# Tanh values of the mixing rounded once and spread to MT's row groups by DMA

## What is computed

```python
xx = x_prev - x
mix = jnp.tanh((x + xx * time_maa_x) @ maa_w1).reshape(b, t, 5, E_MIX)   # E_MIX = 32
mix = jnp.einsum('btfe,fec->fbtc', mix, maa_w2)
mw, mk, mv, mr, mg = mix
xw = x + xx * (time_maa_w + mw)      # and so for k, v, r, g
...
r, k, v = xr @ Wr.T, xk @ Wk.T, xv @ Wv.T
g = silu(xg @ Wg.T)
decay = exp(-exp(time_decay + tanh(xw @ td_w1) @ td_w2))
# a recurrence over time with decay, k, v and r; then a norm by head, times g, @ Wo.T
```

## Time and profile before

| | us |
|---|---|
| median of 3 runs | 3111.87 |
| lowest and highest run | 3108.07, 3113.85 |
| span of the profiled execution | 3113.6 |
| TensorE busy | 2943.4 (95%) |
| VectorE busy | 2445.0 (79%) |
| ScalarE busy | 1976.6 (63%) |
| GpSimd busy | 894.4 (29%) |
| ScalarE's copies into MT (L693), 330 | 135.6 |
| GpSimd's subtractions into MT (L905), 330 | 318.5 |

### The profile page before, as it was taken

The page is one execution under the profiler, slowest core; times in us unless marked ns, Lnnn a source line. Parts: engine busy times, 40 slices in busy tenths (PEclk is TensorE's granted clock), DMA queues, the critical chain, the costliest instruction groups (busy, mean ns, idle before and its releaser), DMA issues.

```text
span 3113.6 us, 102428 instructions
## 1 busy us (share of the span) xinstructions
PE 2943.4 (95%) x40633; PEld 2187.3 (70%) x40633; DVE 2445.0 (79%) x5275; ACT 1976.6 (63%) x4175; POOL 894.4 (29%) x790
## 2 busy tenths in 40 slices
PE   1889999999999999999999999999999999999997
PEld 0667777777777777677777777777777777777775
DVE  8467887787887787787778787778788778788777
ACT  0456676666677666677666667666667666667764
POOL 1223221333222233322233322233322233322222
PEclk9899999999999999999999999999999999999998
DMA  5000000000000000000000000000000000000000
GB/s 212 8 15 22 13 23 19 22 15 22 12 23 19 22 15 22 16 19 19 22 15 22 22 12 19 22 17 21 22 12 23 19 22 15 22 12 23 19 22 14
DMA packets 22823, 73.40 MB, mean 24 GB/s; under 512 B 3105, under 2 KB 3361, under 8 KB 20769
## 3 DMA queue, kind: packets, MB, share of 16 engines
q1 hardware_dynamic: 22432, 67.10, 6.3%
HBM read 50.31 MB, written 16.78 MB: 22 GB/s over the span
## 4 chain that ended last, share of the span: by engine, by line
PE 70%; DVE 19%; issue 6%; ACT 3%; DMA 1%; DVEq 1%; SPq 0%; ACTq 0%; POOLq 0%; POOL 0%
PE psP L402 18%; PE psF L636 11%; PE psP L440 7%; PE psP L611 7%; PE psF L663 6%; DVE HLO L1342 4%; PE psW L479 2%; PE psY L533 2%; PE psY L521 2%; DVE SUMS L1334 2%; PE psW L496 2%; PE psF L652 2%; DVE ARENA L1091 2%; DVE ARENA L1169 1%; DVE ARENA L1279 1%
## 5 line engine op out<-in xcount | busy, mean ns | idle before, releaser
L402 PE MATMUL psP<-ARENA,WALL 128*128 128x256 f32 x3072 | 698.7, 383 | 39.4 <-ACT ARENA L736 39.4
L693 ACT ACTIVATE ARENA<-ARENA 32x512 f32<-32x512 f32 (+3 forms) x1026 | 584.4, 570 | 221.2 <-DVE ARENA L1169 92.4
L402 PEld LDWEIGHTS psP<-ARENA,WALL 128*128 128x128 f32 x3072 | 573.7, 191 | 117.5 <-ACT ARENA L736 42.4
L1342 DVE SCALAR_TENSOR_TENSOR HLO<-GG,FWB,HHI 128x128 f16<-128x128 f32 x1024 | 347.6, 400 | 321.4 <-ACT HHI L864 316.3
L636 PE MATMUL psF<-XHI,WFC 128*128 128x128 f16 x4096 | 488.5, 220 | 1.9 <-DVE ST L1356 1.9
L636 PE MATMUL psF<-XLO,WFC 128*128 128x128 f16 x4096 | 487.1, 220 | 0.0
L905 POOL TENSOR_TENSOR MT<-ARENA 32x256 fp32r<-32x256 f32 x330 | 318.5, 965 | 467.3 <-ACT ARENA L693 438.7
L919 POOL TENSOR_TENSOR ARENA<-ARENA,XT 128x1024 f32<-128x1024 f32 x128 | 278.7, 2178 | 533.9 <-DVE ARENA L1103 533.9
L636 PEld LDWEIGHTS psF<-XHI,WFC 128*128 128x128 f16 x4096 | 398.3, 98 | 37.7 <-issue 32.9
L636 PEld LDWEIGHTS psF<-XLO,WFC 128*128 128x128 f16 x4096 | 402.0, 98 | 17.9 <-issue 10.3
L663 PE MATMUL psF<-WPJ,HHI 128*128 128x512 f16 x1024 | 390.9, 382 | 14.4 <-ACT GG L855 14.4
(11 more groups left out here) (165 smaller groups left out, 5242.1 us busy)
## 6 DMA issues: line engine op xcount, KB each, us to landing
XT<-x_ch SPq DMA_DIRECT2D x33, 520.0 KB, 3.4
ARENA<-x_tok SPq DMA_DIRECT2D x32, 512.0 KB, 3.5
out<-OUT SPq DMA_DIRECT2D x64, 256.0 KB, 2.1
WALL<-w_all SPq DMA_DIRECT2D x5, 1024.0 KB, 15.3
ARENA<-wfc SPq DMA_DIRECT2D x4, 1024.0 KB, 8.0
ARENA<-wpj SPq DMA_DIRECT2D x3, 1024.0 KB, 14.7
GG<-wpj SPq DMA_DIRECT2D x1, 1024.0 KB, 18.7
OUT<-w2a SPq DMA_DIRECT2D x8, 64.0 KB, 14.0
```

The lines of the kernel that those rows point to most:

```text
L402: mm = pe.matmul(psP[:, P.bank(f"{name}{g}"), COLS * c:COLS * (c + 1)], WALL[:, w, k, 128 * (2 * g + c):128 * (2 * g + c + 1)], cc(XF[slot ...
L693: return act.activation(o, i, ACT.Copy)
L1342: e = dve.scalar_tensor_tensor(out=HLO[:, k, :], in0=GG[:, u % 2, 0, 128 * m:128 * (m + 1)], scalar=FWB[:, 0, k:k + 1], in1=HHI[:, k, :], ...
```

## The change

ScalarE keeps the tanh and the two roundings (TMH, TMBH) and makes no copies into MT. GpSimd makes one subtraction of 128 x 256 (TML) and one of 32 x 256 (TMBL). SP issues eight DMAs per tile (`spread`), four of 128 KB from TMH and TML into groups 0 to 3 of MT[0..3], and four of 32 KB from TMBH and TMBL into those of MT[4]. TensorE waits for all four of the first kind before any of blends 0 to 3, and for all four of the second kind before blend 4. For a DMA whose destination has 32 partitions and four blends on each, the source must have the blends of one row next to each other; so GpSimd puts W1's 128 columns in that order once, in the prologue (w1_ordered), from a raw copy in V. TMBH and TMBL move to RM.

```diff
@@ -145,14 +145,15 @@
         A = ARENA1[:, 6144:7168]
         RSX = A.rearrange("p (q n) -> p q n", q=PAIRS)
         K1 = ARENA1[:, 7168:8192]
-        TMA, TMH = K1[:, 0:COLS], K1[:, COLS:2 * COLS]
-        TMB, TMBH = K1[0:MIXR, 2 * COLS:3 * COLS], K1[0:MIXR, 3 * COLS:4 * COLS]
+        TMA, TMH, TML = (K1[:, COLS * i:COLS * (i + 1)] for i in range(3))
+        TMB = K1[0:MIXR, 3 * COLS:4 * COLS]
         KT = ARENA1[:, 7168:8192].rearrange("p (q n) -> p q n", q=PAIRS)
         S = ARENA2[:, 0:512].rearrange("p (c b n) -> p c b n", b=B, c=KC)
         XF = [ARENA2[:, 512 + 1024 * i:1536 + 1024 * i] for i in range(2)]
         YSB, YSQ = XF
         KM = ARENA2[:, 2560:3584]
         RM = ARENA2[:, 3584:4608]
+        TMBH, TMBL = RM[0:MIXR, 0:COLS], RM[0:MIXR, COLS:2 * COLS]
         XTOK = KM.rearrange("p (h c) -> p h c", h=PAIRS)
         D = ARENA2[:, 4608:5632]
         G = ARENA2[:, 5632:6656]
@@ -194,6 +195,7 @@
         RAW = ([ARENA1[:, 2048 * k:2048 * (k + 1)] for k in range(4)] + [ARENA2[:, 2048 * k:2048 * (k + 1)] for k in range(3)]
                + [GG[:, :, :, :].rearrange("p i s n -> p (i s n)")])
 
+        W1RAW = V[:, 1, :].rearrange("p (k n) -> p k n", k=KC)
         W2RAW = (OUT[:, 0:2, :], X1[:, 0:2, :], V[:, 0:1, :])
         psP = ctx.enter_context(nc.psum_tensor("psP", [128, 2, 512], F32))
         psW = ctx.enter_context(nc.psum_tensor("psW", [128, 2, 512], F32))
@@ -215,7 +217,8 @@
         f_stats, f_product = sem("f_read_stats"), sem("f_read_product")
         y_full, y_copied, y_squared = sem("y_full"), sem("y_copied"), sem("y_squared")
         xx_ready, xm_ready, xf_ready = sem("xx_ready"), sem("xm_ready"), sem("xf_ready")
-        tm_rounded, mt_high, mt_low, w2_split = sem("tm_rounded"), sem("mt_high"), sem("mt_low"), sem("w2_split")
+        tm_rounded, tm_rest, w2_split, w1_ordered = sem("tm_rounded"), sem("tm_rest"), sem("w2_split"), sem("w1_ordered")
+        mt_first, mt_last = sem("mt_first_in"), sem("mt_last_in")
         gate_tanh, d_ready = sem("gate_tanh"), sem("d_ready")
         k1_even, k1_odd = sem("k1_even"), sem("k1_odd")
         rb_act, rb_dve = sem("rb_act"), sem("rb_dve")
@@ -262,7 +265,7 @@
                     halves(RM[rows(h), :], n)[1].rearrange("p (c q) n -> p c q n", c=KC))
 
         NPL = len(LEVELS) + 2
-        NWEIGHTS = 8 + 5 * 4
+        NWEIGHTS = 9 + 5 * 4
 
         def over_tiles(eng, attention, feed_forward):
 
@@ -286,7 +289,7 @@
                 sp.dma_start(RAW[4 + k], wpj[:, 2048 * k:2048 * (k + 1)]).then_inc(raw_in[4 + k], 16)
             sp.dma_start(XT[:, :, :], x_ch[0]).then_inc(xt_in, 16)
             sp.dma_start(WALL[:, W_V, :, :], w_all[:, W_V, :, :]).then_inc(values_in, 16)
-            for dst, src in ((W1[:, :, :], w1), (TD1[:, :, :], td1),
+            for dst, src in ((W1RAW, w1[:, :, 0:4 * MIXR]), (W1[:, :, 4 * MIXR:], w1[:, :, 4 * MIXR:]), (TD1[:, :, :], td1),
                              (TD2[0:DECR, :], td2), (TD2[DECR:2 * DECR, :], td2), (WALL[:, W_K, :, :], w_all[:, W_K, :, :])):
                 sp.dma_start(dst, src).then_inc(weights_in, 16)
             for f in range(5):
@@ -296,6 +299,25 @@
                 sp.dma_start(WALL[:, w, :, :], w_all[:, w, :, :]).then_inc(weights_in, 16)
 
 
+            MT32 = MTALL[:, :, :].bitcast(F32)
+
+            def spread(t):
+
+                sp.wait_ge(tm_rounded, 2 * t + 3)
+                for copy in (0, 2):
+                    sp.dma_start(MT32[rows(copy), 0:4, :], TMH).then_inc(mt_first, 16)
+                sp.wait_ge(tm_rest, 2 * t + 3)
+                for copy in (1, 3):
+                    sp.dma_start(MT32[rows(copy), 0:4, :], TML).then_inc(mt_first, 16)
+                sp.wait_ge(tm_rounded, 2 * t + 4)
+                for copy in (0, 2):
+                    sp.dma_start(MT32[rows(copy), 4, :], TMBH).then_inc(mt_last, 16)
+                sp.wait_ge(tm_rest, 2 * t + 4)
+                for copy in (1, 3):
+                    sp.dma_start(MT32[rows(copy), 4, :], TMBL).then_inc(mt_last, 16)
+
+            spread(-1)
+
             def tile(it, first, ffn):
                 if ffn:
                     ffn.late()
@@ -304,6 +326,7 @@
                 sp.dma_start(XT[:, :, :], x_ch[nxt]).then_inc(xt_in, 16)
                 sp.wait_ge(x_full, X.full(it, "kt1"))
                 sp.dma_start(XTOK[:, :, :], x_tok[it]).then_inc(xtok_in, 16)
+                spread(it)
                 if ffn:
                     ffn.finish()
 
@@ -368,14 +391,14 @@
                 return mm
 
             pe.wait_ge(xm_ready, 1)
+            pe.wait_ge(w1_ordered, 1)
             tanh_argument("w1a").then_inc(tm_first, 1)
             tanh_argument("w1b").then_inc(tm_first, 1)
             against_second(1)
 
             def mix(t, f, name, wait_free):
 
-                pe.wait_ge(mt_high, 5 * (t + 1) + f + 1)
-                pe.wait_ge(mt_low, 10 * (t + 1) + 2 * f + 2)
+                pe.wait_ge(mt_first if f < 4 else mt_last, 16 * 4 * (t + 2))
                 lhs, rhs = W2S[:, f, :], MT[f]
                 for g in range(2):
                     wait_free(f"{name}{g}")
@@ -692,27 +715,17 @@
             def copy(o, i):
                 return act.activation(o, i, ACT.Copy)
 
-            def high(t, f):
-
-                src = TMA[rows(f), :] if f < 4 else TMB
-                copy(MT[f][rows(0), :], src)
-                copy(MT[f][rows(2), :], src).then_inc(mt_high, 1)
-
             def mix_high(t, arguments, n):
 
                 act.wait_ge(tm_ready, M.read(t, "w1a"))
-                copy(TMH.bitcast(F32R), TMA[:, :]).then_inc(tm_rounded, 1)
-                high(t, 0)
+                copy(TMH.bitcast(F32R), TMA).then_inc(tm_rounded, 1)
                 act.wait_ge(arguments, n)
                 ps = M_BANKS[M.bank("w1b")]
                 for q in range(4):
                     e = act.activation(TMB[:, CH * q:CH * (q + 1)], ps[MIXR * q:MIXR * (q + 1), 0:CH], ACT.Tanh)
                 e.then_inc(tm_ready, 1)
-                for f in range(1, 4):
-                    high(t, f)
                 act.wait_ge(tm_ready, M.read(t, "w1b"))
-                copy(TMBH.bitcast(F32R), TMB[:, :]).then_inc(tm_rounded, 1)
-                high(t, 4)
+                copy(TMBH.bitcast(F32R), TMB).then_inc(tm_rounded, 1)
 
             act.wait_ge(su_dve, 6)
             act.wait_ge(su_pool, 2)
@@ -741,7 +754,8 @@
                 if not first:
                     act.wait_ge(x_full, X.full(it - 1, "kv1"))
                     act.wait_ge(p_dve, P.read(it - 1, "wo1"))
-                act.wait_ge(mt_low, 10 * (it + 1))
+                act.wait_ge(mt_first, 16 * 4 * (it + 1))
+                act.wait_ge(mt_last, 16 * 4 * (it + 1))
                 for g in range(2):
                     act.wait_ge(p_full, P.full(it, f"k{g}"))
                     src = psP[:, P.bank(f"k{g}"), :]
@@ -884,6 +897,8 @@
             pool.wait_ge(su_pool, 2)
 
             pool.wait_ge(weights_in, 16 * NWEIGHTS)
+            pool.tensor_copy(W1[:, :, 0:4 * MIXR].rearrange("p k (e f) -> p k e f", f=4),
+                             W1RAW.rearrange("p k (f e) -> p k e f", f=4)).then_inc(w1_ordered, 1)
             for i in range(3):
                 if i:
                     pool.wait_ge(w2_split, 2 * i)
@@ -892,21 +907,15 @@
                 pool.wait_ge(w2_split, 2 * i + 1)
                 pool.tensor_tensor(w[64:128, :, :], W2RAW[i][64:128, :, :], w[64:128, :, :].bitcast(F32), ALU.subtract).then_inc(w2_split, 1)
 
-            def mix_low(t, start, end):
+            def mix_low(t):
 
                 pool.wait_ge(tm_rounded, 2 * t + 3)
-                for n in range(start, end):
-                    if n:
-                        pool.wait_ge(mt_low, 10 * (t + 1) + n)
-                    if n == 8:
-                        pool.wait_ge(tm_rounded, 2 * t + 4)
-                    f = n // 2
-                    whole, high = (TMA[rows(f), :], TMH[rows(f), :]) if f < 4 else (TMB, TMBH)
-                    pool.tensor_tensor(MT[f][rows(1 + 2 * (n % 2)), :], whole, high, ALU.subtract).then_inc(mt_low, 1)
-                pool.wait_ge(mt_low, 10 * (t + 1) + end)
+                pool.tensor_tensor(TML.bitcast(F32R), TMA, TMH, ALU.subtract).then_inc(tm_rest, 1)
+                pool.wait_ge(tm_rounded, 2 * t + 4)
+                pool.tensor_tensor(TMBL.bitcast(F32R), TMB, TMBH, ALU.subtract).then_inc(tm_rest, 1)
 
             pool.wait_ge(w2_split, 6)
-            mix_low(-1, 0, 10)
+            mix_low(-1)
 
             def inverse_root(v):
                 return pool.tensor_tensor(v, v, MINUS_HALF.broadcast_to([128, v.shape[1]]), ALU.pow)
@@ -955,8 +964,7 @@
                 pool.wait_ge(s_decayed, it + 1)
                 if ffn:
                     ffn.root_settled()
-                mix_low(it, 0, 2)
-                mix_low(it, 2, 10)
+                mix_low(it)
 
             def row_root(t):
```

## The result

The median is 3124.24 us (3121.19 to 3127.66, 5 runs) against 3111.87 us of the kernel before: ratio 1.0043, interval 1.0030 to 1.0057. The change makes the kernel 12 us slower; forecast was 3110, a little faster, with 3125 as the time of the rival "the transfers come late". The profiled execution has a span of 3124.3 us against 3113.6.

A forecast was written before the change was run, and what follows sets the result against it. The prediction held the kernel bound by a VectorE-to-TensorE chain of 92.6 us a turn: 31 turns x 0, prologue -1.7, tail 0, so 3111.9 - 1.7 = 3110 us; range for 8 in 10, 3104 to 3128.

The forecast's parts named there:

- the transfers come late: Rival: the four DMAs land after 1103.88 and TensorE waits before mix "mw" every tile; 3125 to 3163 us, chance 0.20.
- VectorE's relief: HLO products beside GpSimd's subtractions fall by up to 1.4 us a tile, but VectorE then waits for W_O: gain 0.
- the first rival: Late DMAs into MT stop TensorE before mix "mw" in every tile; 13 to 51 us slower, chance 0.20.
- the prologue's term: Prologue: GpSimd's W1 copy in front lets VectorE's four products in earlier, so TensorE's tanh product starts earlier; -1.7 us.
- the transfers, the only new thing on the way to TensorE: Tile loop, before mix "mw": four DMAs into MT land at 1103.20, ready 1103.3, due 1103.88; cost 0.
- Slack 0.6: Before mix "mw": transfers ready at 1103.3, 0.6 us ahead of the first weight load due at 1103.88.
- The pitch of the issues: SP's four DMA issues in the tile follow each other every 0.45 us, taken from four issued in a row.
- the second brake: SP's low-copy issues wait for GpSimd's TML, done at 1100.17, so they go out at 1100.35 and 1100.80.
- The landing: Each 128 KB copy into MT takes 2.4 us from issue to landing, taken from the 256 KB store.
- The rival's price: Late transfers with a 3.4 us landing: mix "mw" 0.4 us late, 31 x 0.4 = +13 us, 3125; rival's chance 0.20.
- the point of decision: Before mix "mw": transfers are late if landing takes over 2.98 us after the last issue, at a pitch of 0.45.
- the late case: Transfers land too late for mix "mw", making the kernel slower by more than about 6 us; chance 0.20.

The follow-up runs named there:

- e6: The changed kernel with mix "mw" one W_O k step later and the loop-branch prefetch hint on every engine: 3105.61 us, 0.9980 of the kernel before.
- e4: The kernel before with only the change's prologue, W1 by two loads and one GpSimd copy: 3109.92 us, ratio 0.9993.
- e9: The kernel before, one execution, with SBUF-to-SBUF transfers of several forms appended after the last store, singly and in rows; some 40 us added at the end.
- e3: The kernel before with four extra 128 KB transfers per tile from TMH into unused RM, nothing near the mixing waiting for them: 3116.63 us, ratio 1.0021.
- e5: The changed kernel with a hint on every engine that the tile loop's closing branch will be taken: 3119.67 us, 1.0020 of the kernel before.
- e2: The changed kernel with two more 128 KB transfers issued ahead of the low copies and counted by TensorE's wait: 3198.18 us, 1.0284 of the kernel before.
- e7: The changed kernel with the two TMH transfers issued on ScalarE's queue instead of SP's: 3124.67 us, 1.0039 of the kernel before.
- e8: The kernel before with only the loop-branch prefetch hint on every engine: 3112.32 us, ratio 1.0001.

## Where the prediction was right and wrong

**Right.** The turn runs from VectorE's L1282 to TensorE, and the work taken off ScalarE, GpSimd and VectorE is worth nothing in the usual turn: e6 has all of it and a turn of 92.64 us. Two turns of 30 are the exception (0.57 us each, at L1114), which one usual turn could not show. VectorE's relief ends in a wait for W_O, as worked out. The mechanism of the loss was the first rival, with its place, the first weight load of "mw".

**Half right: the prologue's term.** The order is as worked out, and the gain is smaller: the tanh product starts 1.15 us earlier, not 1.7. I priced the copy at 0.69 us and 0.97 more beside VectorE; it took 2.12. VectorE's fourth product ends at 78.47, where I had 78.0. Whether any of it is in the 3124 us no run shows (e4).

**Wrong: the step "the transfers, the only new thing on the way to TensorE".** By my sum the last issue came 1.43 us behind TMH's end and the transfer was there 3.93 us behind it; due was 4.51 us (1103.88 - 1099.37). Slack 0.6. In the changed kernel the last issue comes 1.98 us behind TMH's end (1099.09 - 1097.11) and the weight load could start at 5.29 (1102.40). Lateness 0.78. The difference of 1.36 has two terms:
- *The pitch of the issues*, 0.55 us of it. I took 0.45 us from the earlier trace rows; it is 0.65. The four issues then follow each other without waiting for TML (ready at 1097.91, the second issue ends at 1098.40), which I had as the second brake. SP sets the time, not GpSimd.
- *The landing*, 0.79 us of it. I took 2.4 us from a store of twice the size, because I held a smaller transfer to be no slower. It is 3.19 (the wake-up of 0.12 instead of 0.1 is the rest). e9 divides this: alone the form takes 2.7 to 2.8, and behind three others 3.2. Bytes were the wrong measure.

**Missing: a second deadline.** I asked only when the first weight load of "mw" is due. TensorE's queue has to be through that wait in time for the loop's branch of 3.6 us, which stands behind it, with mk behind the branch. That deadline lies close to the first one and was not in the sum at all: I had read the chain and the busy times, where the branch does not appear as long as it is hidden. The Trainium skill (Runtime: NRT & Kernel Launch, Instruction fetch mechanics) says that a taken branch to a target outside the pages at hand forces a fetch by DMA before execution can go on. By that rule the trace agrees: between 1101.9 and 1105.6 in the kernel before, while TensorE's branch runs, the queue for instructions moves one packet of 16 KB, and none in the 3.9 us ahead of it; the branch takes 3.6 us, 0.36 with the hint, and 4.83 beside the transfers of e3. No run here changes the length of the loop, which would show the rule itself.

**The size of the loss.** Lateness is not loss one to one. The weight load was 0.78 us late, but W_O's second half starts 4.62 us behind the first (1103.13 - 1098.51) instead of 4.17 (1104.94 - 1100.77): 0.45 us. The chain of before:

```profile
1104.47 0.23 PE psX L383 x2
...
1104.94 3.43 PE psP L611 x8
```

Normally the first load runs 0.59 us ahead of psX's product (1103.88 and 1104.47); here it has 0.01 us (1102.40 and 1102.41). So the product starts only 0.20 us late, 3.90 us behind W_O's start for 3.70, and its pair takes 0.50 us for 0.23. Then 0.10 us come back at mk (1.50 for 1.60 us to psF, e5), which leaves 0.35, as e5 has it with 0.36; the branch adds 0.27 in the mean (1.77 - 1.50; 0.26 by the turns). 0.36 + 0.26 = 0.62 us a turn, 17 us in 28 turns, less 6 at the start. The rival's price for a landing of 3.4 us was 0.4 us late and +13 us; the measured +12 is near it by chance, since it leaves out the pitch, the branch and the start. The stated range, 3104 to 3128, holds 3124 only because it was stretched to this rival.

**The choice that decided.** Of two rows for a kind of transfer that no row shows, 2.4 and 3.4 us, I took the one that kept the slack, for its bytes. With the pitch of 0.45 the point of decision was 2.98 us, between them, so the rows did not decide, and 0.20 was too low a chance for the late case.

## What to carry to other kernels

When copies on an engine are replaced by DMAs, ask when the copies were ready and when the reader's queue, not only the reader, needs them: an in-order queue that is held at a wait also holds the weight loads and the branch behind it, which had been done ahead for nothing. Price a transfer by one of the same form and with the same company, partitions on both sides and neighbours in the queue, not by its bytes. And before moving work off an engine, look whether anyone waits for that engine: here 4 and 8 us a tile were taken from two engines for which nobody waited in 28 turns of 30.

## What the runs showed of the hardware

- TensorE's closing branch of a loop with some 2,500 instructions in its body (40633 matmuls and as many weight loads over 32 tiles) takes 3.6 us, that of the other engines 0.05 (median of 30 each); with the prefetch hint TensorE's takes 0.36 us.
- A transfer inside SBUF of 128 KB lands in 2.0 us from 128 partitions to 128, and in 2.7 to 2.8 us from 128 to 32 with four rows each; four of the latter in a row in up to 3.2, and the last of six in a row took 3.8 us (e2).
- Issues of such transfers in a row on one queue follow each other mostly every 0.65 us in three forms (e9), where four loads in the prologue took 0.45 us each; a second queue (e7) does not bring the last landing forward.
- VectorE's sum L1282 takes 0.71 us when GpSimd's first subtraction starts 0.55 to 0.57 us ahead of it (before, e4), and 0.80 to 0.82 when it starts 0.45 to 0.49 ahead (e3, e8).
- Two executions with the same prologue had TensorE's clock at different levels around 100 us, worth 3 us (10.11 against 7.14 us for the same 32 matmuls).
